# Both feed-forward blocks of a hybrid transformer kernel: inputs mixed with the previous token ahead of the products, residual sums on GpSimd

## The chip, the cores and the metric

The kernel runs on one core of a Trainium2 chip. The metric is the device time of one execution in microseconds (us), where less is better. The engines are named as the profile names them: PE (TensorE), its weight loads PEld, DVE (VectorE), ACT (ScalarE), POOL (GpSimd) and SP (SyncE, which issues the transfers). Each runs its own list of instructions in order, and they wait for each other by semaphores.

## The reference

The input x has 2 sequences of 2048 tokens with 128 features, all float32. Four blocks follow each other, each added to x after a layernorm: causal attention with one head of 128 and rotary embedding, the FFN, a linear attention with 16 heads of 64 and a decaying state, and the same FFN with the same weights again. The change is to the FFN:

```python
def ffn(x, W_r, W_k, W_v, mu_r, mu_k):
    x_prev = concatenate([zeros, x[:, :-1, :]], axis=1)    # the token before
    xr = mu_r * x + (1 - mu_r) * x_prev                    # mu: one factor per feature
    xk = mu_k * x + (1 - mu_k) * x_prev
    r = sigmoid(xr @ W_r.T)
    k_act = square(relu(xk @ W_k.T))
    return r * (k_act @ W_v.T)
```

## The kernel before

The program is a row of phases: projections, attention, the first FFN (ffn_phase, lines 782 to 994), and the linear phase (linear_phase, from line 1314), into whose last steps the last FFN (class LastFfn, from line 1179) is woven. At the end of a phase all engines meet before the next one starts. X holds all tokens in SBUF from start to end.

An FFN works on 8 groups of 512 tokens (4 tiles of 128), even groups from the first sequence, odd ones from the second. A group goes through these steps, which both FFNs have under the same names:

- moments (DVE, lines 92 to 100), roots (POOL, 102 to 107: variance plus eps, then the power of -0.5) and normalize (DVE, 109 to 113: four pieces) give the normed tokens, two groups of buffers.
- turn (PE): four transposes to a PSUM bank, so that features lie in the partitions. copy_x (ACT) copies it to xT, 513 columns wide: column 0 is the last token of the group before in the same sequence, kept by a one-column copy. So the token before is the same buffer shifted by a column.
- copy_x also rounds xT to x_hi, and low_part (POOL) subtracts x_hi from xT to get x_lo. The keys are exact to more than the fast format fp32r by three products hi*hi, hi*lo, lo*hi.
- keys (PE): W_k is held twice, times mu and times 1 - mu (FfnWeights.vector, 761 to 770, at the attention's start, with wk_hi and wk_lo made from both). For each of the two shifts there are three matmuls over 512 columns, six in all. receptance (PE): four blocks of 128 tokens, for each one a float32 product with x and W_r*mu and one with the token before and W_r*(1 - mu), eight in all. A float32 matmul shows as two passes in the profile.
- tanh (ACT) gives the gate from the receptance, as sigmoid is half of 1 + tanh of the half. square (ACT): Relu and then Square of the keys. values (PE): four float32 products with W_v.
- output (DVE): gated = (tanh + 1) * values, then X = gated + X. In the last FFN, SP stores each group's tokens when its sum is there (eight transfers of 256 KB).

The first FFN runs the groups in slots. In slot k, DVE has normalize(k+1), moments(k+2), output(k-2); PE has turn(k), receptance(k-1), values(k-2), keys(k-1); ACT has copy_x(k), tanh(k-1), square(k-1) and some exponentials for tables of the linear phase (eight each in slots 0 and 1, four each in slots 6 and 7); POOL has low_part(k), roots(k+2), and in slot 7 the product of a table of 128x1024 (line 1145). In slot 8, DVE first scales the output weights (line 1174) and norms the first two tiles for the linear phase. Each of the four PSUM results has two banks.

The last FFN has one bank for each result, borrowed from the linear attention, and its order is written out by hand on each engine (lines 1702 to 1733, 1887 to 1912, 2070 to 2090, 2190 to 2199). Between its steps stand those of the linear phase's last token tile: square_u (ACT) and sum_squares (PE) sum the outputs' squares, add_totals, turn_totals and gather_totals bring them to invert_totals (POOL, a power of -0.5), turn_scales, copy_scales and spread_scales bring the factors back, scale_u, high_u and low_u apply and split, project_out (PE, 24 matmuls), copy_y, turn_y and residual add them to X. Groups 6 and 7 hold the last tile of their sequence, so their moments can't start before that residual.

## Time and profile before

| | us |
|---|---|
| time before, median of 3 runs | 908.69 (906.55 to 910.41) |
| the profiled execution's own time | 905.67 |
| its span, first to last instruction | 901.5 |
| PE, DVE, ACT, POOL busy | 814.4, 556.2, 570.5, 584.7 |
| mean granted clock of PE | 0.981 |

The span is what the trace covers; the time of the same execution holds some 4 us around it. Busy times are sums over the span, and a busy engine is one with an instruction at work, a blocked one included. A granted clock of 1.00 is TensorE's full speed (2.4 GHz), 0.5 its lower level (1.2 GHz).

### The profile page before, as it was taken

Reading aid. Unit: us, or ns where it says so; the run is one execution under the profiler, and the core shown is the slowest. Engines: PE = TensorE matmul, PEld = TensorE weight load, DVE = VectorE, ACT = ScalarE, POOL = GpSimd, SP = SyncE. Lnnn points to the kernel's source line nnn. Section 1 sums busy time; section 2 is a strip of 40 time slices with the busy share of each in tenths; the row PEclk is TensorE's granted clock in tenths of the full one; section 3 lists DMA queues with packets and bytes.
Section 4 is the critical chain, followed back from the end, with each engine's and each line's share of the span. In section 5 each row is a group of like instructions: output and inputs, shape, how many; then the busy total and the mean of one; then the engine's idle time right before and its main releaser. Section 6 shows DMA issues by size and latency. Waiting matters only on the chain.

```text
span 901.5 us, 31429 instructions
## 1 busy us (share of the span) xinstructions
PE 814.4 (90%) x13280; PEld 707.7 (79%) x13280; DVE 556.2 (62%) x1296; ACT 570.5 (63%) x1202; POOL 584.7 (65%) x514
## 2 busy tenths in 40 slices
PE   4958998999797799999999999999999999996977
PEld 3647997899696687888788888888888887875866
DVE  3976666566684356567467466567467566567463
ACT  4746554655565666767767767767767767664544
POOL 4983211320445888977977967977977977977332
PEclk9988999999998899999999999999999999999999
DMA  5101000100100000000000000000000000000011
...
DMA packets 19417, 12.38 MB, mean 14 GB/s; under 512 B 7760, under 2 KB 18768, under 8 KB 19024
## 3 DMA queue, kind: packets, MB, share of 16 engines
...
## 4 chain that ended last, share of the span: by engine, by line
PE 55%; POOL 4%; DVE 4%; issue 3%; ACT 2%; DVEq 0%; POOLq 0%; ACTq 0%
PE la_ps L1465 9%; PE la_ps L1467 8%; PE la_ps L1466 8%; PE la_o_ps L1528 4%; PE la_o_ps L1544 4%; PE la_s_ps L1558 3%; PE la_ps L1575 3%; PE la_ps L1509 3%; PE la_ps L1496 2%; PE la_ps L1609 2%; PE la_ps L1610 2%; PE la_ps L1611 2%; DVE la_u L1765 1%; POOL la_scale L2141 1%; PE la_ps L1598 1%
## 5 line engine op out<-in xcount | busy, mean ns | idle before, releaser
L2109 POOL TENSOR_TENSOR la_coef<-la_ssk,lt_mhalf 128x32 f32<-128x32 f32 x16 | 87.1, 5442 | 70.2 <-DVE la_ssk L1782 70.2
L1465 PE MATMUL la_ps<-la_x_hi,w_hi 128*128 128x256 f32 x384 | 115.0, 300 | 1.8 <-ACT la_v L1922 1.7
L1467 PE MATMUL la_ps<-la_x_hi,w_lo 128*128 128x256 f32 x384 | 107.5, 280 | 0.4 <-issue 0.4
L1466 PE MATMUL la_ps<-la_x_lo,w_hi 128*128 128x256 f32 x384 | 107.3, 279 | 0.0
L2141 POOL TENSOR_TENSOR la_scale<-la_scale,lt_mhalf 128x32 f32<-128x32 f32 x16 | 99.9, 6241 | 6.8 <-DVE la_scale L1758 6.8
L1805 DVE TENSOR_TENSOR lt_state<-la_s_ps,la_faded 128x512 f32<-128x512 f32 x62 | 42.6, 686 | 70.0 <-PE la_o_ps L1544 57.6
L1465 PEld LDWEIGHTS la_ps<-la_x_hi,w_hi 128*128 128x128 f32 x384 | 72.2, 188 | 11.2 <-issue 6.2
L713 ACT ACTIVATE at_probs<-at_s_ps,at_ntop 128x512 f32<-128x512 f32 (+2 forms) x80 | 49.0, 623 | 46.5 <-DVE at_ntop L655 46.4
L598 PE MATMUL at_o_ps<-V,at_probsT 128*128 128x128 f32 x544 | 74.5, 277 | 3.2 <-DVE at_probsT L507 2.0
L531 POOL CAST at_q_hi<-qk_hi 128x128 fp32r<-128x128 f32 x32 | 9.4, 294 | 104.6 <-PE at_s_ps L572 102.2
L598 PEld LDWEIGHTS at_o_ps<-V,at_probsT 128*128 128x128 f32 x544 | 68.9, 192 | 6.4 <-ACT at_probsT L729 2.3
L1466 PEld LDWEIGHTS la_ps<-la_x_lo,w_hi 128*128 128x128 f32 x384 | 72.3, 188 | 0.7
L1467 PEld LDWEIGHTS la_ps<-la_x_hi,w_lo 128*128 128x128 f32 x384 | 72.2, 188 | 0.6 <-issue 0.6
L1943 ACT ACTIVATE la_gate<-la_ps,lt_bias_g 128x256 f32<-128x256 f32 x128 | 50.1, 483 | 34.7 <-PE la_ps L1467 34.7
L2135 POOL TENSOR_TENSOR la_faded<-lt_state,lt_decay_s 128x512 f32<-128x512 f32 x62 | 64.2, 1046 | 7.3 <-DVE lt_state L1805 7.1
L1742 DVE TENSOR_TENSOR la_pT<-la_ps,lt_decay 128x512 f32<-128x512 f32 x64 | 41.1, 683 | 41.7 <-PE la_ps L1509 41.7
L2127 POOL TENSOR_TENSOR la_k<-la_k,lt_decay_k 128x1024 f32<-128x1024 f32 x32 | 61.0, 1906 | 4.8 <-ACT n_xn L1992 4.8
L1465 PE MATMUL la_ps<-w_hi,la_x_hi 128*128 128x512 f32 x128 | 57.1, 446 | 7.1 <-POOL la_x_lo L2100 4.3
L2119 POOL TENSOR_TENSOR la_v<-la_v,la_coef 128x1024 f32<-128x1024 f32 x32 | 60.3, 1905 | 1.3
L1943 ACT ACTIVATE la_f<-la_ps,lt_bias_f 128x256 f32<-128x256 f32 x128 | 51.6, 473 | 13.7 <-PE la_ps L1467 12.4
L1922 ACT ACTIVATE la_k<-la_ps 128x512 f32<-128x512 f32 x64 | 38.4, 600 | 30.5 <-PE la_ps L1467 27.7
L1544 PE MATMUL la_o_ps<-la_qdT,lt_state 64*64 64x64 f32 x2048 | 45.7, 222 | 8.7 <-issue 5.9
...
## 6 DMA issues: line engine op xcount, KB each, us to landing
...
```

The source lines that it names most:

```text
L598: mm = eng.matmul(o_ps[n % 2][:, 0:P], probsT[:, (BLK[n] + j) % 2, t * P:(t + 1) * P], V[:, bass.ds(b * NT + kt, 1), :], start=(kt == 0), ...
L713: eng.activation(probs[:, n % 2, j * G:j * G + width], s_ps[:, k * G:k * G + width], ACT.Exp, bias=ntop[:, n % 2, 1:2], scale=1.0 / C, acc ...
L1465: eng.matmul(out, l_hi, r_hi, start=True, stop=False)
L1466: eng.matmul(out, l_hi, r_lo, start=False, stop=False)
L1467: return eng.matmul(out, l_lo, r_hi, start=False, stop=True)
L1544: mm = eng.matmul(o_ps[h % 2][rows, part(i, c)], state[own, b, h // 2, :], qdT[own, b, h // 2, chunk(c)], start=False, stop=True, skip_gro ...
L1943: act = eng.activation(where[:, c, :], ps[bank][:, r * W:(r + 1) * W], ACT.Tanh, bias=bias[:, c:c + 1], scale=0.5)
L2109: eng.tensor_tensor(coef[:, :], ssk[:, :], mhalf[:, :], ALU.pow).then_inc(s["coef_step"], 1)
L2119: eng.tensor_tensor(own, own, over_d(coef[:, b * H:(b + 1) * H]), ALU.mult).then_inc(s["vb_ready"], 1)
L2127: eng.tensor_tensor(own, own, over_d(decay_k[:, :]), ALU.mult).then_inc(s["kd_ready"], 1)
L2135: eng.tensor_tensor(faded[:, b, :, :], state[:, b, :, :], over_e, ALU.mult).then_inc(s["faded_second" if c else "faded_first"], 1)
L2141: eng.tensor_tensor(scale[:, :, :], scale[:, :, :], powers, ALU.pow).then_inc(s["scale_step"], 1)
```

## The change

- FfnWeights keeps W_k and W_r as they are. The products with mu and 1 - mu go (four operations on DVE), wk_hi and wk_lo have half the size, and 1 - mu (rest) is kept as a factor per feature.
- A new ACT step, rests, makes xk and xr as the token before times 1 - mu, by two scaled copies of 512 columns. A new DVE step, mix, adds x times mu to each. xk is split by high_part (ACT, was part of copy_x) and low_part (POOL, or DVE for group 2 of the last FFN); both are 512 columns wide.
- keys has three matmuls and not six, receptance four and not eight.
- output is split into gate (DVE) and residual, which is on POOL, apart from groups 0 and 7 of the last FFN, where DVE does it. Relu and Square work in one buffer, and the gate writes over the tanh.
- Both FFNs are one class, Ffn. In a slot of the first one DVE has normalize(k+1), mix(k), moments(k+2), gate(k-2); ACT has copy_x(k), rests(k), tanh(k-1), high_part(k), square(k-1) and the exponentials; POOL has low_part(k), roots(k+2), residual(k-2).
- In the last FFN the order is rewritten on each engine. low_part(1) is now behind invert_totals on POOL, keys(1), turn(3), values(1), receptance(2) and keys(2) are ahead of turn_scales on PE.

```diff
     def vector(self, eng):
-        w, mu, rest, wk, wr = self.w, self.mu, self.rest, self.wk, self.wr
         eng.wait_ge(self.loaded, 32)
-        eng.tensor_scalar(rest[:, :], mu[:, :], -1.0, 1.0, ALU.mult, ALU.add).then_inc(self.rest_ready, 1)
-        eng.tensor_scalar(wk[:, 0, :], w[:, 1, :], mu[:, 1:2], None, ALU.mult).then_inc(self.scaled, 1)
-        eng.wait_ge(self.rest_ready, 1)
-        eng.tensor_scalar(wk[:, 1, :], w[:, 1, :], rest[:, 1:2], None, ALU.mult).then_inc(self.scaled, 1)
-        eng.tensor_scalar(wr[:, 0, :], w[:, 0, :], mu[:, 0:1], None, ALU.mult).then_inc(self.scaled, 1)
-        eng.tensor_scalar(wr[:, 1, :], w[:, 0, :], rest[:, 0:1], None, ALU.mult).then_inc(self.scaled, 1)
-        eng.tensor_scalar(self.wv[:, :], w[:, 2, :], 0.5, None, ALU.mult).then_inc(self.scaled, 1)
+        eng.tensor_scalar(self.rest[:, :], self.mu[:, :], -1.0, 1.0, ALU.mult, ALU.add).then_inc(self.scaled, 1)
+        eng.tensor_scalar(self.wv[:, :], self.w[:, 2, :], 0.5, None, ALU.mult).then_inc(self.scaled, 1)
     def scalar(self, eng):
-        eng.wait_ge(self.scaled, 2)
-        eng.activation(self.wk_hi[:, :, :], self.wk[:, :, :], ACT.Copy).then_inc(self.wk_hi_ready, 1)
+        eng.wait_ge(self.loaded, 32)
+        eng.activation(self.wk_hi[:, :], self.w[:, 1, :], ACT.Copy).then_inc(self.wk_hi_ready, 1)
     def gpsimd(self, eng):
         eng.wait_ge(self.wk_hi_ready, 1)
-        eng.tensor_tensor(self.wk_lo[:, :, :], self.wk[:, :, :], self.wk_hi[:, :, :].bitcast(F32),
-                          ALU.subtract).then_inc(self.wk_lo_ready, 1)
...
+class Ffn:
...
+    def keys(self, eng, g):
+        w, hi, lo = self.weights, self.x_hi[:, g % 2, :], self.x_lo[:, g % 2, :]
+        eng.wait_ge(self.lo_ready[g % 2], g // 2 + 1)
+        ps = self.bank(eng, "k", g, self.k_pos_ready)
+        eng.matmul(ps[:, :], w.wk_hi[:, :], hi, start=True, stop=False)
+        eng.matmul(ps[:, :], w.wk_lo[:, :], hi, start=False, stop=False)
+        eng.matmul(ps[:, :], w.wk_hi[:, :], lo, start=False, stop=True).then_inc(self.k_full, 1)
+    def receptance(self, eng, g):
+        eng.wait_ge(self.xr_ready, g + 1)
+        ps = self.bank(eng, "r", g, self.r_ready)
+        for j in range(GT):
+            part = slice(j * P, (j + 1) * P)
+            mm = eng.matmul(ps[:, part], self.xr[:, g % 2, part], self.weights.wr, start=True, stop=True)
+        mm.then_inc(self.r_full, 1)
...
+    def mix(self, eng, g):
+        x, mu = self.xT[:, g % 2, 1:1 + G], self.weights.mu
+        for k, (own, ready) in enumerate(((self.xk, self.xk_ready), (self.xr, self.xr_ready))):
+            eng.wait_ge(self.rest_ready, 2 * g + k + 1)
+            eng.scalar_tensor_tensor(own[:, g % 2, :], x, mu[:, 1 - k:2 - k], own[:, g % 2, :], ALU.mult, ALU.add).then_inc(ready, 1)
+    def gate(self, eng, g):
+        eng.wait_ge(self.r_ready, g + 1)
+        eng.wait_ge(self.o_full, g + 1)
+        own, banks = self.r_act[:, g % 2, :], self.banks["o"]
+        eng.scalar_tensor_tensor(own, own, 1.0, banks[g % len(banks)][:, :], ALU.add, ALU.mult).then_inc(self.gated_ready, 1)
+    def copy_x(self, eng, g):
+        b, banks = g % 2, self.banks["xt"]
+        eng.wait_ge(self.xt_full, g + 1)
+        if g == 0:
+            eng.wait_ge(self.carried, 1)
+        if g >= 2:
+            eng.wait_ge(self.xk_ready, g - 1)
+            eng.wait_ge(self.xr_ready, g - 1)
+            eng.activation(self.xT[:, b, 0:1], self.xT[:, b, G:G + 1], ACT.Copy).then_inc(self.carried, 1)
+            eng.wait_ge(self.carried, g)
+        eng.activation(self.xT[:, b, 1:1 + G], banks[g % len(banks)][:, :], ACT.Copy).then_inc(self.xt_ready, 1)
+    def rests(self, eng, g):
+        b, rest = g % 2, self.weights.rest
+        eng.wait_ge(self.xt_ready, g + 1)
+        if g >= 2:
+            eng.wait_ge(self.lo_ready[g % 2], g // 2)
+        eng.activation(self.xk[:, b, :], self.xT[:, b, 0:G], ACT.Copy, scale=rest[:, 1:2]).then_inc(self.rest_ready, 1)
+        if g >= 2:
+            eng.wait_ge(self.r_full, g - 1)
+        eng.activation(self.xr[:, b, :], self.xT[:, b, 0:G], ACT.Copy, scale=rest[:, 0:1]).then_inc(self.rest_ready, 1)
+    def high_part(self, eng, g):
+        eng.wait_ge(self.xk_ready, g + 1)
+        if g >= 2:
+            eng.wait_ge(self.k_full, g - 1)
+        eng.activation(self.x_hi[:, g % 2, :], self.xk[:, g % 2, :], ACT.Copy).then_inc(self.hi_ready, 1)
...
+    def low_part(self, eng, g):
+        eng.wait_ge(self.hi_ready, g + 1)
+        eng.tensor_tensor(self.x_lo[:, g % 2, :], self.xk[:, g % 2, :], self.x_hi[:, g % 2, :].bitcast(F32),
+                          ALU.subtract).then_inc(self.lo_ready[g % 2], 1)
+    def residual(self, eng, g):
+        eng.wait_ge(self.gated_ready, g + 1)
+        eng.tensor_tensor(self.tokens(g), self.r_act[:, g % 2, :].rearrange("p (t c) -> p t c", t=GT), self.tokens(g),
+                          ALU.add).then_inc(self.x_ready[g % 2], 1)
...
+        @block.vector
+        def _(eng):
+            for k in range(N + 2):
+                if k == N:
+                    tables.vector(eng)
+                    for g in range(2):
+                        eng.wait_ge(ffn.x_ready[g], 1)
+                    next_norm.first_vector(eng)
+                if has(k + 1) and k + 1 >= 2:
+                    ffn.normalize(eng, k + 1)
+                if has(k):
+                    ffn.mix(eng, k)
+                if has(k + 2):
+                    ffn.moments(eng, k + 2)
+                if has(k - 2):
+                    ffn.gate(eng, k - 2)
+        @block.scalar
+        def _(eng):
+            for k in range(N + 2):
+                if has(k):
+                    ffn.copy_x(eng, k)
+                    ffn.rests(eng, k)
+                if has(k - 1):
+                    ffn.tanh(eng, k - 1)
+                if has(k):
+                    ffn.high_part(eng, k)
+                if has(k - 1):
+                    ffn.square(eng, k - 1)
...
+                if has(k):
+                    ffn.low_part(eng, k)
+                if has(k + 2):
+                    ffn.roots(eng, k + 2)
+                if k == N:
+                    next_norm.first_gpsimd(eng)
+                if has(k - 2):
+                    ffn.residual(eng, k - 2)
...
             for m in STEPS[:-1]:
                 step(m)
+            eng.wait_ge(s["u_ready"], 2 * B * NT)
+            ffn.receptance(eng, 0)
             eng.wait_ge(up_read[0], B * NT)
             ffn.keys(eng, 0)
             sum_squares(NT, "su")
             ffn.turn(eng, 2)
             turn_totals(NT)
-            eng.wait_ge(s["u_ready"], 2 * B * NT)
-            ffn.receptance(eng, 0)
-            ffn.keys(eng, 1)
             ffn.values(eng, 0)
             ffn.receptance(eng, 1)
+            ffn.keys(eng, 1)
             ffn.turn(eng, 3)
+            ffn.values(eng, 1)
+            ffn.receptance(eng, 2)
+            ffn.keys(eng, 2)
             turn_scales(NT)
             for j in range(4):
                 spread_scales(NT, j)
-            ffn.keys(eng, 2)
-            ffn.receptance(eng, 2)
-            project_out(NT)
-            ffn.values(eng, 1)
             ffn.values(eng, 2)
-            turn_y(NT)
             ffn.receptance(eng, 3)
             ffn.keys(eng, 3)
+            project_out(NT)
             ffn.turn(eng, 4)
             ffn.values(eng, 3)
-            for g in range(4, ffn.GROUPS):
-                if g + 1 < ffn.GROUPS:
-                    ffn.turn(eng, g + 1)
-                ffn.receptance(eng, g)
-                if g > 4:
-                    ffn.values(eng, g - 1)
-                ffn.keys(eng, g)
-            ffn.values(eng, ffn.GROUPS - 1)
+            turn_y(NT)
+            ffn.receptance(eng, 4)
+            ffn.turn(eng, 5)
+            ffn.keys(eng, 4)
+            ffn.values(eng, 4)
+            ffn.receptance(eng, 5)
+            ffn.turn(eng, 6)
+            ffn.keys(eng, 5)
+            ffn.values(eng, 5)
+            ffn.receptance(eng, 6)
+            ffn.turn(eng, 7)
+            ffn.keys(eng, 6)
+            ffn.receptance(eng, 7)
+            ffn.values(eng, 6)
+            ffn.keys(eng, 7)
+            ffn.values(eng, 7)
...
+            ffn.mix(eng, 1)
             ffn.normalize(eng, 3)
-            ffn.output(eng, 0)
+            ffn.moments(eng, 4)
+            ffn.mix(eng, 2)
+            ffn.gate(eng, 0)
+            ffn.residual(eng, 0)
+            ffn.low_part(eng, 2)
+            ffn.moments(eng, 5)
+            ffn.mix(eng, 3)
+            ffn.gate(eng, 1)
             for j in range(4):
                 scale_u(NT, j)
             for j in range(4):
                 low_u(NT, j)
-            ffn.moments(eng, 4)
-            ffn.output(eng, 1)
             ffn.normalize(eng, 4)
-            ffn.moments(eng, 5)
+            ffn.normalize(eng, 5)
+            ffn.gate(eng, 2)
+            ffn.mix(eng, 4)
             residual(NT)
-            ffn.normalize(eng, 5)
             taken(eng, NT, "yt")
             ffn.moments(eng, 6)
-            ffn.output(eng, 2)
-            ffn.output(eng, 3)
+            ffn.moments(eng, 7)
+            ffn.gate(eng, 3)
+            ffn.mix(eng, 5)
             ffn.normalize(eng, 6)
-            ffn.moments(eng, 7)
-            ffn.output(eng, 4)
             ffn.normalize(eng, 7)
-            for g in range(5, ffn.GROUPS):
-                ffn.output(eng, g)
+            ffn.gate(eng, 4)
+            ffn.mix(eng, 6)
+            ffn.gate(eng, 5)
+            ffn.mix(eng, 7)
+            ffn.gate(eng, 6)
+            ffn.gate(eng, 7)
+            ffn.residual(eng, 7)
...
+                    ffn.rests(eng, 1)
+                    ffn.high_part(eng, 0)
             for m in STEPS[:-1]:
                 step(m)
             square_u(LAST, 1)
+            ffn.tanh(eng, 0)
             ffn.square(eng, 0)
             ffn.copy_x(eng, 2)
-            ffn.tanh(eng, 0)
+            ffn.rests(eng, 2)
+            ffn.high_part(eng, 1)
+            ffn.tanh(eng, 1)
             ffn.square(eng, 1)
-            ffn.tanh(eng, 1)
             ffn.copy_x(eng, 3)
+            ffn.high_part(eng, 2)
+            ffn.rests(eng, 3)
+            ffn.tanh(eng, 2)
+            ffn.square(eng, 2)
             copy_scales(NT)
+            ffn.high_part(eng, 3)
             for j in range(4):
                 high_u(NT, j)
-            ffn.square(eng, 2)
-            ffn.tanh(eng, 2)
-            copy_y(NT)
             ffn.tanh(eng, 3)
             ffn.square(eng, 3)
+            copy_y(NT)
             ffn.copy_x(eng, 4)
+            ffn.rests(eng, 4)
+            ffn.high_part(eng, 4)
             for g in range(4, ffn.GROUPS):
                 if g + 1 < ffn.GROUPS:
                     ffn.copy_x(eng, g + 1)
+                    ffn.rests(eng, g + 1)
                 ffn.tanh(eng, g)
                 ffn.square(eng, g)
+                if g + 1 < ffn.GROUPS:
+                    ffn.high_part(eng, g + 1)
...
+                    eng.wait_ge(up_full[0], B * NT)
                     ffn.low_part(eng, 0)
-                    ffn.low_part(eng, 1)
             step(STEPS[0])
             tables.gpsimd_clear(eng)
             for m in STEPS[1:-1]:
                 step(m)
             invert_totals(NT)
-            ffn.low_part(eng, 2)
+            ffn.low_part(eng, 1)
             ffn.roots(eng, 4)
+            ffn.roots(eng, 5)
             ffn.low_part(eng, 3)
-            ffn.roots(eng, 5)
+            ffn.residual(eng, 1)
+            ffn.low_part(eng, 4)
+            ffn.residual(eng, 2)
             ffn.roots(eng, 6)
-            ffn.low_part(eng, 4)
             ffn.roots(eng, 7)
-            for g in range(5, ffn.GROUPS):
-                ffn.low_part(eng, g)
+            ffn.residual(eng, 3)
+            ffn.low_part(eng, 5)
+            ffn.residual(eng, 4)
+            ffn.low_part(eng, 6)
+            ffn.residual(eng, 5)
+            ffn.low_part(eng, 7)
+            ffn.residual(eng, 6)
```

## Rows read from the trace of the kernel before

**Rows 1.** The page: busy time by engine; shares of the chain that ended last.

```profile
PE 814.4 (90%) x13280; PEld 707.7 (79%) x13280; DVE 556.2 (62%) x1296; ACT 570.5 (63%) x1202; POOL 584.7 (65%) x514
...
PE 55%; POOL 4%; DVE 4%; issue 3%; ACT 2%; DVEq 0%; POOLq 0%; ACTq 0%
```

**Rows 2.** Windows: stretch; length; busy us of PE, PEld, DVE, ACT, POOL; clock; DMA.

```profile
235.50:280.60 45.10, 38.81 (x272) 33.91 (x272) 35.84 (x111) 30.36 (x73) 22.17 (x27) 1.00 0.07 13
280.60:285.00 4.40, 3.74 (x11) 2.88 (x12) 0.00 (x0) 2.59 (x5) 2.91 (x8) 0.52 0.02 6
```

**Rows 3.** Timeline, first FFN, PE: start, duration, engine, line, output<-inputs, count [idle before].

```profile
247.46 0.40 PE L973 MATMUL f_r_ps<-fw_wr,f_xT 128*128 128x128 f32 x2
...
249.26 1.06 PE L981 MATMUL f_o_ps<-fw_wv,f_k_act 128*128 128x128 f32 x8
...
250.07 0.47 PE L963 MATMUL f_k_ps<-f_x_hi,fw_wk_hi 128*128 128x512 f32 x1
...
251.56 0.75 PE L955 MATMUL f_xt_ps<-const,n_xn 128*128 128x128 f32 x4
...
252.14 0.40 PE L973 MATMUL f_r_ps<-fw_wr,f_xT 128*128 128x128 f32 x2
```

**Rows 4.** Timeline, first FFN, DVE and POOL: one turn, the first and last normalize.

```profile
240.29 2.07 DVE L112 TENSOR_SCALAR n_xn<-X,n_mv,n_rstd 128x128 f32<-128x128 f32 x4 [3.52 <-POOL n_rstd L107]
...
247.16 0.86 DVE L94 BATCH_NORM_STATS2 n_stats<-X 128x6 f32<-128x128 f32 x4
...
248.80 1.01 POOL L107 TENSOR_TENSOR n_rstd<-n_rstd,n_mhalf 128x4 f32<-128x4 f32 x1
...
249.78 1.29 POOL L855 TENSOR_TENSOR f_x_lo<-f_xT,f_x_hi 128x513 fp32r<-128x513 f32 x1
249.91 2.01 DVE L112 TENSOR_SCALAR n_xn<-X,n_mv,n_rstd 128x128 f32<-128x128 f32 x4 [0.18 <-POOL n_rstd L107]
...
263.98 2.02 DVE L112 TENSOR_SCALAR n_xn<-X,n_mv,n_rstd 128x128 f32<-128x128 f32 x4 [0.18 <-POOL n_rstd L107]
```

**Rows 5.** Groups by form, POOL (whole span), ACT (first FFN): busy us, mean ns.

```profile
L239 POOL TENSOR_TENSOR qkv_rot<-qkv_by_cos,qkv_by_sin 128x512 f32<-128x512 f32 x16 | 24.3, 1534 | 0.5 <-issue 0.3 <-DVE qkv_by_sin L278 0.2
...
L914 ACT ACTIVATE f_x_hi<-f_xT 128x513 fp32r<-128x513 f32 x8 | 5.1, 634 | 0.3
...
L1128 ACT ACTIVATE lt_decay<-lt_lag,lt_rate 128x64 f32<-128x64 f32 x16 | 4.0, 333 | 0.0
```

**Rows 6.** Timeline, end of the first FFN.

```profile
269.90 1.43 DVE L883 TENSOR_TENSOR X<-f_gated,X 128x512 f32<-128x512 f32 x1
...
270.75 2.82 POOL L1145 TENSOR_TENSOR lt_decay<-lt_decay,lt_strict 128x1024 f32<-128x1024 f32 x1
...
271.26 2.94 DVE L1174 TENSOR_SCALAR lt_w_out<-lt_w_out,lt_norm_w 128x1024 f32<-128x1024 f32 x1
...
280.68 0.57 PE L1452 MATMUL la_ps<-const,n_xn 128*128 128x128 f32 x2 [3.60 <-PEq L788]
```

**Rows 7.** Timeline, the weights' products at the attention's start, DVE.

```profile
67.03 0.38 DVE L765 TENSOR_SCALAR fw_wk<-fw_w,fw_mu 128x128 f32<-128x128 f32 x1
...
68.06 0.29 DVE L648 TENSOR_TENSOR at_s_ps<-at_s_ps,const 128x128 f32<-128x128 f32 x1
```

**Rows 8.** Timeline, the last FFN, by engine: DVE, ACT, POOL, PE.

```profile
846.11 2.14 DVE L1797 SCALAR_TENSOR_TENSOR la_u<-la_gate,la_u 128x1024 f32<-128x1024 f32 x1
...
868.97 1.11 DVE L112 TENSOR_SCALAR n_xn<-X,n_mv,n_rstd 128x128 f32<-128x128 f32 x4
...
898.07 0.69 DVE L1270 TENSOR_TENSOR X<-f_gated,X 128x512 f32<-128x512 f32 x1
...
846.23 1.06 ACT L2006 ACTIVATE la_sq<-la_u 128x1024 f32<-128x1024 f32 x1 [0.42 <-DVE la_u L1791]
...
850.36 5.46 POOL L2141 TENSOR_TENSOR la_scale<-la_scale,lt_mhalf 128x32 f32<-128x32 f32 x1 [3.20 <-DVE la_scale L1758]
...
863.49 0.39 PE L1609 MATMUL la_ps<-la_u_hi,lt_w_out_hi 128*128 128x256 f32 x1 [1.16 <-DVE la_u_lo L1771]
```

400 lines of the change are left out of this document (112 added, 288 removed).

## The prediction

> **What bounds the kernel now.** I read the page first. PE is busy 90% of the span, and it also has 55% of the chain of waits that ended last [rows 1]. A reader could stop there and price the change by PE's saving. But the change touches two stages only, some 45 us after the attention (the first FFN) and the last 50 us, so I went on to the stretches of time. In the first FFN PE is busy 38.81 of 45.10 us, DVE 35.84, ACT 30.36, POOL 22.17, at full granted clock [rows 2]. The timeline of one group shows PE without a gap: receptance starts at 247.46, values at 249.26, keys at 250.07, the next turn at 251.56, the next receptance at 252.14, so 4.68 us a group [rows 3]. The same timeline shows a second bound at par with it, a loop between DVE and POOL: moments start on DVE at 247.16, the power of the roots runs on POOL from 248.80, and the next normalize starts at 249.91, 2.75 us behind the moments. Its four pieces take 2.01 us, though four undisturbed ones take 1.11 [rows 4, 8]: POOL's low_part started at 249.78 with 1.29 us, just ahead of them, and the first piece had to sit it out. 2.75 + 2.0 is 4.75: the normalize of a group waits for the one before it as much as for PE.
>
> **The first FFN, part by part.** PE: receptance goes from 8 to 4 matmuls, keys from 6 to 3. Receptance took 1.80 us and keys 1.49 [rows 3], so 0.90 and 0.70 us go, 1.6 us a group, and PE has about 3.1 us of work in it. ACT: two scaled copies (rests) come in, x_hi moves behind the mix as high_part. One 128x513 SBUF copy takes 634 ns [rows 5], and independent ones follow each other by about 0.55 (estimate); ACT goes from some 3.0 to 4.1 us a group. DVE: two mixes come in, the residual sum goes out. The nearest row is the residual sum of the same size, 0.69 us [rows 8]; back to back I take 1.25 us for both mixes (bounds 1.2, and 2.5 if each meets a POOL operation). POOL takes the residual: the nearest row is the 128x512 sum of two SBUF tensors at L239, 1534 ns in the mean with disturbance [rows 5], low_part has 1.29 undisturbed; I take 1.27 (bounds 1.05 to 1.6).
>
> Now the loop. DVE's order becomes normalize(k+1), mix(k), moments(k+2), gate(k-2). The roots of k+2 wait for moments(k+2), normalize(k+2) waits for the roots, and the mix stands between normalize and moments. So the loop is normalize 1.03 (start to start of four undisturbed pieces and what follows, inside the 1.11 of [rows 8]) + mix 1.25 + the 2.75 of [rows 4] = 5.03 us. Two things are added. POOL's residual(k-2) comes right behind the roots, its gate being done by then (0.7 us behind the moments, where the roots take 1.4), so it has started when the normalize arrives and costs it 1.17, as low_part does today. And low_part(k) now waits for mix and high_part: it ends about 0.1 us after the moments, ahead of the roots on POOL. That is 6.3 us for a full turn, against 4.75. PE (3.1) and ACT (4.1) fit within it and save nothing.
>
> In time: today normalize(2) starts at 240.29 and normalize(7) at 263.98, five turns of 4.74 later [rows 4]. After: mix(0) can't start before ACT has copied and scaled group 0 and low_part(0) moves back with it, so normalize(2) starts about 241.7. The next turn is free of a residual (5.15); the third waits for ACT, whose eight exponentials of a slot (x16 in 4.0 us, [rows 5]) now stand ahead of the rests (6.1); three turns of 6.3 follow: normalize(7) at 271.9, +7.9.
>
> The end of the stage: mix(7) waits for rests(7), which stand on ACT behind high_part(6), square(5) and four exponentials: 278.7. high_part and low_part(7) follow until 281.6. Then POOL has residual(5), the 128x1024 product at L1145, the roots for the next phase, and residuals 6 and 7. L1145 took 2.82 from 270.75, of which DVE's residual at 269.90 (1.43, itself held until POOL was done) was ahead for 0.54; so 2.3. DVE's L1174 took 2.94, held till L1145 ended [rows 6]; it works 0.65. Summed: residual(5) to 283.4 (behind L1174), L1145 to 285.7, roots of 1.0 and 0.9 to 287.9, normalizes to 288.6, gates 6 and 7 to 290.1, residual(7) at 290.7 to 291.9. Today the next phase's first matmul is at 280.68 [rows 6], 0.3 us behind the last residual; both end in a barrier. So +11.5 us. Bounds: +6 if no residual blocks and the end hides on ACT's side, +14 if mixes are blocked too.
>
> **Weights.** Four products of weights with mu leave DVE, 67.03 to 68.06 without wv and rest, just ahead of the attention's first mask [rows 7], where PE stands idle: -0.8 us (bounds -1.0 and 0). The wk_hi and wk_lo operations halve beside other work: nothing.
>
> **The last FFN.** Its groups lie between steps of the linear phase's last chain. I followed the new order by hand with the durations above. The sums of x: rests(0) and mix(0) fall in idle time of ACT and DVE. After copy_x(1), ACT now also has rests(1) and high_part(0) ahead of square_u: 846.23 becomes 846.8 [rows 8]. low_part(0), today long done, can start only at 846.95. DVE's gate_u, which today starts at 846.11 and is held to 2.14 us by a low_part [rows 8], is then first, and holds low_part(0) until 847.3; it ends at 848.6. keys(0) stands ahead of the sum of squares on PE and waits for it, then takes 0.8. So the power of the totals starts on POOL at 852.3, not 850.36 [rows 8]: 2.0 late.
>
> The larger delay is behind it. low_part(1) stood ahead of invert_totals on POOL; now it stands behind, so it waits out the 5.46 us power and its two followers (to 858.45) and ends at 859.75. PE holds keys(1), turn(3), values(1), receptance(2) and keys(2) ahead of turn_scales. keys(1) ends 860.65, Relu and Square on ACT 862.0, values(1) and receptance(2) 863.9, and keys(2) waits for low_part(2) on DVE (copy_x(3) and high_part(2) are behind the Square) until 864.1. turn_scales follows at 864.9, the spread at 866.7, scale_u and low_u to 872.2: project_out starts at 872.25, not 863.49 [rows 8], +8.8.
>
> Given back: with groups 0 to 2 done and group 3 nearly so, what comes behind is shorter. turn_y ends 877.05, rests and mix of group 4 hold residual(NT) until 878.7, moments 6 and 7 to 881.65, roots to 883.9, normalizes to 888.0 (residual(3) and low_part(5) get in between their pieces). turn(7) stands behind values(5) and receptance(6): 892.0. From there one chain: copy 1.5 with the start, rests and mix to 894.9, high_part behind tanh(6) and square(6) 896.9, low_part 898.3, keys 899.2, Relu and Square 900.5, values 901.6, gate and residual 903.1. Today the last residual ends at 898.76 [rows 8]: +4.3 us. Bounds: -5 if PE's 1.6 us per group count here after all, +9.
>
> PE idles some 5.5 us before keys(1). An idle of 3.60 us before 280.68 today has a granted clock of 0.52 behind it, the lower level of 1.2 GHz [rows 2, 6]. keys(1), values(1) and receptance(2) would then take up to twice their time, and about 1.5 us of it falls on the chain; I add that (bounds 0 and 3).
>
> **Sum.** +11.5 - 0.8 + 4.3 + 1.5 = +16.5. The profiled execution had a span of 901.5 and a time of 905.67, 3 us under the median of 908.69; the sum gives a span of 918 and 922.2 by that execution, 925 by the median. I take 924.
>
> **Rivals.**
> A, PE was the bound, 897: in the tail DVE's gate waits for PE, and PE is busy 90% [rows 1]. If each of the last seven groups gives back 1.6 us (11 us) and the first FFN falls to DVE's own work of 4.4 us a group (normalize 1.1, mixes 1.3, moments 1.3, gate 0.7; -1.5), the kernel gets faster by 12. It decides if the moments' loop has slack, which [rows 4] speak against: the normalize starts as soon as the roots are there. 9%.
> B, the residual on POOL doesn't hold the normalize up: turns of 5.1, the first FFN at +6, in all +11: 920. Against it is the 2.01 for 1.11 [rows 4, 8]. 15%.
> The Trainium skill, "Perfetto Trace Analysis", section "Optimizing Scalar/DVE Operations", warns that moving work between GpSimd and DVE may not help as they share an SBUF port; by it B does not come about and the sum stays at +16.5 and not +11, and the 2.01 agrees.
> C, the clock: PE is busy half of each turn in the first FFN. If the grant falls to 1.2 GHz there and through the tail, PE needs 6.2 us a group, at par with the loop, and keys, values and turns lengthen the closing chains: +7 more, 932. For it is the 0.52 of [rows 2], against it that PE's idle time in a turn is cut into pieces of under 2 us by turn, receptance, values and keys. 10%.
> D, loss and gain cancel: the first FFN +5, the tail -5, 909. 11%.
> The forecast itself: 55%, its own range 917 to 930.
>
> Half a per cent, 4.5 us, is what a measurement here can tell from no change. Faster: A and a little of D, 0.10. Same: the middle of D, 0.07. Slower: 0.83. The range of 910 to 932 leaves out A, half of D and the upper end of C.
>
> **What would show it.** In the first FFN: normalize starts 6.3 us apart, residuals on POOL starting right at the roots' end with a first normalize piece of 1.2 to 1.3 beside them, PE idle near half. Its end near 292. In the tail: low_part(1) behind the power, PE idle from 854 to 860, project_out near 872 to 874, the last residual near 903. It is wrong if the normalizes start under 5 us apart, or if project_out starts before 866.

## The result, and the profile after

| | before | after |
|---|---|---|
| time, median of 4 runs each | 907.62 us (904.08 to 910.41) | 929.11 us (927.22 to 929.91) |
| profiled execution: time, span | 905.67, 901.5 | 927.22, 924.9 |
| PE, DVE, ACT, POOL busy | 814.4, 556.2, 570.5, 584.7 | 808.7, 563.8, 589.5, 599.4 |
| mean granted clock of PE | 0.981 | 0.958 |

The changed kernel takes 1.0237 of the time before (95% interval 1.0205 to 1.0269): 21 us more. Run again later beside the kernel before, it had 926.55 against 905.46 us, 1.0241 (1.0210 to 1.0271). The forecast was 924 with 910 to 932.

The page says where not to look: PE's busy time fell by 5.7 us although half of its products in both FFNs went, and PE's share of the chain that ended last rose from 55% [rows 1] to 57%.

```profile
PE 808.7 (87%) x13104; PEld 696.5 (75%) x13104; DVE 563.8 (61%) x1311; ACT 589.5 (64%) x1234; POOL 599.4 (65%) x527
...
PE 57%; DVE 3%; ACT 3%; issue 3%; POOL 2%; DVEq 0%; POOLq 0%; ACTq 0%
```

Two marks cut the 23.4 us that the span grew by: x_lo, POOL's first operation on the tokens of the linear phase, and gate_o, DVE's first operation on the last outputs of the linear attention. The first x_lo of the linear phase starts at 292.00 instead of 282.09: +9.9, of which the attention's first mask gives back 0.5 (67.56 instead of 68.06, [rows 7]), so the first FFN itself is +10.4. The last step's gate_o starts at 854.09 instead of 844.91: +9.2, so the linear phase gave back 0.7. From that gate_o to the end of the last residual it is 68.06 us instead of 53.85: +14.2. Nearly all lies in the two stretches that the change touches.

The timeline of DVE in the first FFN, to be read against [rows 4] (start, duration, engine, line, operation, shape, and in brackets idle time and its releaser; L112 is normalize, L863 mix, L94 the first half of moments, L869 gate):

```profile
246.22 1.11 DVE L112 TENSOR_SCALAR n_xn<-X,n_mv,n_rstd 128x128 f32<-128x128 f32 x4 [1.51 <-POOL n_rstd L107]
...
252.35 1.99 DVE L112 TENSOR_SCALAR n_xn<-X,n_mv,n_rstd 128x128 f32<-128x128 f32 x4 [1.09 <-POOL n_rstd L107]
254.26 0.74 DVE L863 SCALAR_TENSOR_TENSOR f_xk<-f_xT,fw_mu,f_xk 128x512 f32<-128x512 f32 x1
254.92 0.74 DVE L863 SCALAR_TENSOR_TENSOR f_xr<-f_xT,fw_mu,f_xr 128x512 f32<-128x512 f32 x1
255.59 0.86 DVE L94 BATCH_NORM_STATS2 n_stats<-X 128x6 f32<-128x128 f32 x4
...
256.78 0.66 DVE L869 SCALAR_TENSOR_TENSOR f_r_act<-f_r_act,f_o_ps 128x512 f32<-128x512 f32 x1
258.38 1.99 DVE L112 TENSOR_SCALAR n_xn<-X,n_mv,n_rstd 128x128 f32<-128x128 f32 x4 [0.94 <-POOL n_rstd L107]
```

And POOL beside it (L923 is low_part, L107 the roots' power, L928 the residual sum):

```profile
255.74 1.27 POOL L923 TENSOR_TENSOR f_x_lo<-f_xk,f_x_hi 128x512 fp32r<-128x512 f32 x1 [2.26 <-ACT f_x_hi L899]
...
257.25 1.02 POOL L107 TENSOR_TENSOR n_rstd<-n_rstd,n_mhalf 128x4 f32<-128x4 f32 x1
258.24 1.27 POOL L928 TENSOR_TENSOR X<-f_r_act,X 128x512 f32<-128x512 f32 x1
```

One turn is 258.38 - 252.35 = 6.03 us, and it can be added up from the starts: normalize to mix 1.91, both mixes to moments 1.33, moments to the next normalize 2.79. Before it was 4.7 [rows 4]. The residual sum starts at 258.24, just ahead of the normalize, and the four pieces take 1.99 us; at 246.22, with no sum on POOL, they take 1.11.

The last FFN, PE (L1449 is the sum of squares, L829 opens keys(1), L846 is values: of group 0 at 862.12, of group 1 at 873.89, of groups 4, 5 and 7 in the last three lines; L1472 is the spread, L1483 opens project_out):

```profile
859.33 1.89 PE L1449 MATMUL la_ps<-la_sq,lt_pick 128*32 128x256 f32 x16
...
862.12 1.06 PE L846 MATMUL la_o_ps<-fw_wv,f_k_act 128*128 128x128 f32 x8
...
870.90 0.79 PE L829 MATMUL la_s_ps<-f_x_hi,fw_wk_hi 128*128 128x512 f32 x1 [5.34 <-POOL f_x_lo L923]
...
873.89 2.07 PE L846 MATMUL la_o_ps<-fw_wv,f_k_act 128*128 128x128 f32 x8 [0.49 <-ACT f_k_act L915]
...
880.25 1.21 PE L1472 MATMUL la_ps<-la_scT,lt_spread 128*128 128x256 f32 x8 [1.40 <-ACT la_scT L1858]
...
885.80 0.39 PE L1483 MATMUL la_ps<-la_u_hi,lt_w_out_hi 128*128 128x256 f32 x1 [1.86 <-DVE la_u_lo L1652]
...
898.02 1.59 PE L846 MATMUL la_o_ps<-fw_wv,f_k_act 128*128 128x128 f32 x8 [3.19 <-ACT f_k_act L915]
...
906.07 2.08 PE L846 MATMUL la_o_ps<-fw_wv,f_k_act 128*128 128x128 f32 x8 [3.22 <-ACT f_k_act L915]
...
918.78 1.84 PE L846 MATMUL la_o_ps<-fw_wv,f_k_act 128*128 128x128 f32 x8 [1.35 <-ACT f_k_act L915]
```

Here two things are to be seen: the wait of 5.34 us for low_part(1) behind the power, and durations that vary for one and the same work: the eight matmuls of values take 1.06 us at 862.12 and 2.07 at 873.89. The windows say why (stretch, length, busy us and count of PE, PEld, DVE, ACT, POOL, then the granted clock, DMA share, GB/s):

```profile
860.00:870.00 10.00, 4.29 (x34) 2.73 (x26) 7.75 (x22) 3.92 (x8) 6.74 (x4) 0.84 0.01 2
870.00:880.00 10.00, 7.46 (x28) 6.19 (x28) 3.75 (x13) 5.56 (x11) 4.03 (x5) 0.59 0.09 27
880.00:890.00 10.00, 7.89 (x62) 7.41 (x63) 7.54 (x17) 5.67 (x12) 2.52 (x2) 1.00 0.09 26
890.00:900.00 10.00, 4.79 (x31) 4.07 (x30) 8.81 (x30) 6.47 (x12) 7.30 (x8) 0.93 0.10 28
900.00:910.00 10.00, 6.78 (x32) 6.30 (x31) 3.87 (x7) 4.25 (x8) 4.09 (x4) 0.67 0.17 52
910.00:925.00 15.00, 6.83 (x34) 5.06 (x32) 3.48 (x5) 6.01 (x11) 2.83 (x3) 0.73 0.18 52
```

Before, the clock was 1.00 in every window from 840 to 890, as in this one:

```profile
870.00:880.00 10.00, 7.66 (x58) 6.95 (x57) 8.02 (x36) 5.18 (x10) 3.67 (x5) 1.00 0.25 72
```

After, it is low for most of 870 to 880 (0.59) and of 900 to 910 (0.67), and for part of all other windows but one. Ahead of gate_o it is low for a while in both kernels (0.81 from 830 to 840 before, 0.66 from 840 to 850 after); no run prices that. Note the trap in these rows: PE's busy time in 870 to 880 is 7.46 us for 28 matmul records, and in 880 to 890 7.89 for 62. A slow PE looks busy.

### The profile page after: what moved, and what is told of

Read it like the earlier page. It is cut to its first block, busy times and chain, and to the rows that moved or that the text cites. A ratio compares the mean times of both kernels' runs of the same rounds, so it can differ in the third digit from the quotient of the medians.

```text
span 924.9 us, 31149 instructions
## 1 busy us (share of the span) xinstructions
PE 808.7 (87%) x13104; PEld 696.5 (75%) x13104; DVE 563.8 (61%) x1311; ACT 589.5 (64%) x1234; POOL 599.4 (65%) x527
## 4 chain that ended last, share of the span: by engine, by line
PE 57%; DVE 3%; ACT 3%; issue 3%; POOL 2%; DVEq 0%; POOLq 0%; ACTq 0%
PE la_ps L1339 10%; PE la_ps L1340 8%; PE la_ps L1341 8%; PE la_o_ps L1402 4%; PE la_o_ps L1418 4%; PE la_ps L1449 3%; PE la_s_ps L1432 3%; PE la_ps L1383 3%; PE la_ps L1370 2%; PE la_ps L1483 2%; PE la_ps L1484 2%; PE la_ps L1485 2%; DVE la_u L1646 1%; PE la_ps L1472 1%; PE la_o_ps L846 1%
## 5 line engine op out<-in xcount | busy, mean ns | idle before, releaser
L1836 ACT ACTIVATE la_f<-la_ps,lt_bias_f 128x256 f32<-128x256 f32 x128 | 51.5, 472 | 13.8 <-PE la_ps L1341 12.4
L923 POOL TENSOR_TENSOR f_x_lo<-f_xk,f_x_hi 128x512 fp32r<-128x512 f32 x15 | 19.1, 1273 | 60.0 <-ACT f_x_hi L899 60.0
```

The source lines that it names most:

```text
L1836: act = eng.activation(where[:, c, :], ps[bank][:, r * W:(r + 1) * W], ACT.Tanh, bias=bias[:, c:c + 1], scale=0.5)
```

## The experiments

Ratios are to runs of the kernel before on the same chip. "Tail" is the time from the last step's gate_o to the end of the last residual in the profiled execution (before 53.85, after 68.06, after once more 68.00). Each kernel's theory is quoted as it stood before the run.

### One half at a time

`old_first` has the first FFN as before and the last one as changed:

```
-    ffn_phase(nc, X, const, weights, norm_1, tables, norm_2)
+    ffn_phase(nc, X, const, weights.split, norm_1, "f1_", tables=tables, next_norm=norm_2)
```

> The first FFN as it was, the last FFN as changed; the weights are made in both forms, some 0.8 us more on VectorE at the attention phase's start. Theory (where the traces put the time): the last FFN alone costs 13 to 14 us, so the time is that of before plus 14 to 15, 921 to 923. Rival (the sum of the prediction: 5.8 us for the last FFN and the clock): 913 to 915. A third: a part of the changed tail's loss comes from the pressure of both changes together, and this kernel shows less than 10.

Measured: 919.28 us against 905.28, ratio 1.0165 (1.0139 to 1.0191).

`old_last` has the first FFN as changed and the last one as before:

> The first FFN as changed, the last FFN as it was. Theory: the first FFN costs what its own stretch shows, 9.5 to 10 us, and nothing of it comes back later: 917 to 918. Rival: what the first FFN loses is given back in the linear phase or its tail, under 5 us: 908 to 913. With the kernel above the two losses should add up to the whole, 21 to 23 us; if they don't, the halves act on each other.

Measured: 916.33 against 905.28, ratio 1.0127 (1.0095 to 1.0159). Both kernels make the weights in both forms. normalize(2) starts at 242.50 instead of 240.29 in the one, at 243.64 instead of the changed kernel's 241.06 in the other, so 2.2 and 2.6 us are lost ahead of either FFN, more than the 0.8 us expected. The first mask is no later than before (68.00 and 67.76), so they are lost within the attention phase: from its first mask to its last it takes 152.2 and 152.3 us, where the kernels before and after have 150.1 and 150.3. The granted clock is 0.83 there from 150 to 160 in both, and 1.00 in the kernels before and after. It doesn't take the weights in two forms: `filled` (below) has the changed kernel's weights and attention, and shows the same, 152.0 us. The window of the changed kernel and that of `filled`:

```profile
150.00:160.00 10.00, 8.20 (x54) 6.78 (x55) 7.99 (x36) 5.49 (x16) 3.67 (x12) 1.00 0.02 5
```

```profile
150.00:160.00 10.00, 8.07 (x47) 7.02 (x47) 7.50 (x34) 4.58 (x14) 3.66 (x12) 0.83 0.01 2
```

As they stand, the halves come to 14.0 + 11.1 = 25.1 us, against 21 to 22 for the whole. Without the 2.2 and 2.6 they come to 11.8 + 8.5 = 20.3, so the losses add within their intervals, as far as one profile of each can say. The tail is 68.17 us in `old_first`: nearly all of its loss is made by the last FFN alone, and not by how late it starts. It is 55.48 in `old_last`, whose last FFN is as before. That is 1.6 us over the 53.85 of before, all of it behind residual(NT), where the clock is 0.85 from 880 to 890: a tail of the same code differs by so much from one kernel to the next. The rival of 5.8 us for the last FFN and the clock falls.

### The clock in the tail

The next kernel is the changed one with matmuls that nothing reads, on PE where it stood idle:

```
+    def fill(self, eng, what, g, read, n):
+        ps = self.bank(eng, what, g, read)
+        for j in range(n):
...
+            eng.matmul(ps[:, part], self.weights.wv[:, :], self.const[:, C_IDENT:C_IDENT + P], start=True, stop=True)
...
+            ffn.fill(eng, "k", 1, ffn.k_pos_ready, 24)
             ffn.keys(eng, 1)
```

> The changed kernel with matmuls of 128x128 that nothing reads, put in the last FFN on TensorE where it stood idle (each in a PSUM bank that the next product overwrites; the output is unchanged). Theory: TensorE's clock fell to 0.59 to 0.74 in four stretches of the tail because it had little to do, and this cost 5 to 9 us: the granted clock is over 0.9 in 860 to 920, values(1) takes 1.06 us and not 2.07, and the time is 920 to 924. Rival: the low clock lies beside longer chains on VectorE and ScalarE and costs under 2 us: 927 to 930. A third: the added matmuls stand in the way of the real ones and make it slower, 930 to 934.

Measured: 926.33 against 905.28, ratio 1.0240 (1.0210 to 1.0270), no gain in the time. The trace shows the clock at 1.00 from 850 to 910, as wanted, and a tail of 65.08 us, 3.0 less than in the changed kernel. It isn't more because the added matmuls run past the moment at which the real inputs are there. And 1.7 us of the gain are lost again in the attention phase, at the clock of 0.83 shown above. So the same kernel with fewer of them:

```
-            ffn.fill(eng, "k", 1, ffn.k_pos_ready, 24)
+            ffn.fill(eng, "k", 1, ffn.k_pos_ready, 20)
-            ffn.fill(eng, "xt", 4, ffn.xt_ready, 12)
+            ffn.fill(eng, "xt", 4, ffn.xt_ready, 5)
-            ffn.fill(eng, "o", 4, ffn.gated_ready, 20)
+            ffn.fill(eng, "o", 4, ffn.gated_ready, 8)
...
```

> As the kernel with matmuls that nothing reads, with fewer of them. There the granted clock was 1.00 from 850 to 910 and values(1) took 1.16 us, and still the ratio was 1.024, as without them. But they stood in the way in places: project_out started 1.5 us after its last input, values(4) 2.5 us and values(5) 1.1 us after square's end, receptance(7) 1.5 us after mix. Here the counts are cut so that they end before the inputs do. Theory (the clock's fall costs 5 to 8 us, which the waits took back): ratio 1.015 to 1.018 to before. Rival (the clock's fall costs 1 to 3 us, since the products at half speed stood beside ScalarE's and VectorE's chains): 1.020 to 1.023.

Measured: 919.17 against 905.16, ratio 1.0164 (1.0141 to 1.0188), and a tail of 59.93 us instead of 68.06. Its windows, its sum of squares (L1456) and its values(1) (L853):

```profile
850.00:860.00 10.00, 8.41 (x179) 6.46 (x177) 5.47 (x11) 7.03 (x15) 1.29 (x1) 1.00 0.01 2
860.00:870.00 10.00, 9.09 (x79) 8.59 (x76) 7.75 (x22) 3.61 (x7) 7.83 (x6) 1.00 0.10 28
870.00:880.00 10.00, 7.69 (x58) 6.73 (x58) 6.52 (x18) 8.22 (x16) 5.43 (x5) 1.00 0.01 2
880.00:890.00 10.00, 9.54 (x79) 9.11 (x78) 7.32 (x20) 5.35 (x10) 1.04 (x1) 1.00 0.09 26
890.00:900.00 10.00, 8.52 (x62) 7.13 (x61) 9.50 (x28) 7.21 (x14) 8.11 (x9) 1.00 0.19 54
900.00:910.00 10.00, 7.42 (x59) 6.67 (x58) 3.54 (x6) 6.15 (x12) 4.02 (x4) 1.00 0.18 52
```

```profile
858.99 1.07 PE L1456 MATMUL la_ps<-la_sq,lt_pick 128*32 128x256 f32 x16
...
872.05 1.16 PE L853 MATMUL la_o_ps<-fw_wv,f_k_act 128*128 128x128 f32 x8 [0.91 <-ACT f_k_act L922]
```

No work was taken out and no order changed, only idle time of PE filled, and 8.1 us went from the tail, some 6.6 us (0.0073 of the time) from the kernel. The low clock costs the tail that much. The first form shows how narrow the gap is: with its misplaced matmuls (project_out 1.5 us late, values(4) 2.5, values(5) 1.1, receptance(7) 1.5) the tail kept 3.0 of these 8.1 us.

### The order in the tail

```
             ffn.normalize(eng, 3)          # VectorE
+            ffn.low_part(eng, 1)
             ffn.moments(eng, 4)
...
             invert_totals(NT)              # GpSimd
-            ffn.low_part(eng, 1)
             ffn.roots(eng, 4)
```

> The changed kernel with one operation of the tail moved: low_part(1) from GpSimd behind the power of 128x32 (5.9 us) to VectorE behind normalize(3) (0.7 us). Theory: keys(1) waited 5.3 us for it and everything up to turn_scales, project_out and residual(NT) stood behind keys(1) on TensorE; keys(1) starts at about 866, turn_scales at the power's end near 870, and the last residual comes 7 to 9 us earlier: 920 to 922. Rival: the clock's fall and the chain of ScalarE take most of it back: 925 to 929.

Measured: 916.73 against 905.28, ratio 1.0129 (1.0095 to 1.0163), some 10 us less than the changed kernel; tail 59.86, 8.2 us less. The rest lies ahead of gate_o, where the edit changes nothing: it starts at 852.91 instead of 854.09. In its timeline, PE:

```profile
864.84 0.50 PE L829 MATMUL la_s_ps<-f_x_hi,fw_wk_hi 128*128 128x512 f32 x1 [0.47 <-DVE f_x_lo L923]
...
872.37 1.21 PE L1472 MATMUL la_ps<-la_scT,lt_spread 128*128 128x256 f32 x8 [1.40 <-ACT la_scT L1859]
...
877.92 0.39 PE L1483 MATMUL la_ps<-la_u_hi,lt_w_out_hi 128*128 128x256 f32 x1 [1.86 <-DVE la_u_lo L1652]
```

keys(1) starts 11.9 us behind gate_o (852.91 here) instead of 16.8, project_out 25.0 instead of 31.7. One operation of 0.7 us, moved, gave more than the wait of 5.34 us in front of it. By keys(1) it has given 4.9; the next 1.7 come from values(1) and receptance(2), which take 1.13 and 1.06 us and not 2.07 and 1.92. The granted clock is at 1.00 again from 860 to 890 without any added matmul:

```profile
860.00:870.00 10.00, 6.53 (x50) 5.51 (x47) 9.75 (x28) 6.91 (x13) 7.85 (x5) 1.00 0.04 11
870.00:880.00 10.00, 6.74 (x50) 5.85 (x49) 9.39 (x26) 6.64 (x12) 5.00 (x5) 1.00 0.15 42
880.00:890.00 10.00, 4.91 (x38) 4.20 (x37) 7.25 (x29) 6.80 (x14) 5.20 (x6) 1.00 0.09 26
```

With `filled_less`, where the same idle time is filled, this shows that the idle time in front of keys(1) is what brought the clock down behind it.

### The order in the first FFN

```
                 if has(k + 1) and k + 1 >= 2:
                     ffn.normalize(eng, k + 1)
-                if has(k):
-                    ffn.mix(eng, k)
                 if has(k + 2):
                     ffn.moments(eng, k + 2)
+                if has(k):
+                    ffn.mix(eng, k)
```

with roots(k+2) ahead of low_part(k) on GpSimd in the same way.

> The changed kernel with two pairs exchanged in each slot of the first FFN: VectorE's moments(k+2) ahead of mix(k), GpSimd's roots(k+2) ahead of low_part(k). Theory: a turn is 6.0 us because moments(k+2) to the next normalize holds mix(k) (1.4 us) ahead of the chain moments, roots, normalize; with mix beside roots a turn is 4.9 to 5.3 us and the phase 5 to 6 us shorter, the time 921 to 924 where the changed kernel has 927 to 929. Rival: VectorE is full with or without the order (its own instructions with the blocked normalize are 5.7 us a group), a turn stays at 5.8 to 6.0 and the time within 2 us. A third: low_part behind roots makes keys late, and TensorE and ScalarE then set the turn, 6 us or more.

Measured: 928.08 against 905.16, ratio 1.0245 (1.0209 to 1.0280): no gain in the time, and not quite for one of the reasons given. Its timeline, POOL and DVE:

```profile
256.67 1.26 POOL L923 TENSOR_TENSOR f_x_lo<-f_xk,f_x_hi 128x512 fp32r<-128x512 f32 x1
256.80 2.98 DVE L112 TENSOR_SCALAR n_xn<-X,n_mv,n_rstd 128x128 f32<-128x128 f32 x4 [0.39 <-POOL n_rstd L107]
257.90 1.28 POOL L928 TENSOR_TENSOR X<-f_r_act,X 128x512 f32<-128x512 f32 x1
...
259.70 0.86 DVE L94 BATCH_NORM_STATS2 n_stats<-X 128x6 f32<-128x128 f32 x4
...
261.75 1.41 POOL L107 TENSOR_TENSOR n_rstd<-n_rstd,n_mhalf 128x4 f32<-128x4 f32 x1
...
263.26 2.97 DVE L112 TENSOR_SCALAR n_xn<-X,n_mv,n_rstd 128x128 f32<-128x128 f32 x4 [0.39 <-POOL n_rstd L107]
```

With low_part behind the roots, both of POOL's 128x512 operations stand beside the normalize, whose pieces now take 2.98 us. The turn is 6.46 us, not 5. The mix left the chain (1.33 us), and two things came into it: the second operation on POOL (1.0 us), and roots that take longer beside the mixes. Their power takes 1.41 us and not 1.02, and from the moments to the next normalize it is 3.56 us and not 2.79. DVE is idle for 0.39 us of such a turn, so the rival that VectorE is full was close.

The phase as a whole still got shorter, by 0.6 us from the attention's last mask to x_lo (73.5 instead of 74.1), because the first normalizes start earlier. The time does not show it: the attention phase before it took 1.5 us more in this profile (151.8, at 0.83 from 150 to 160).

### The residual sum in the first FFN

```
                 if has(k - 2):
                     ffn.gate(eng, k - 2)            # VectorE
+                    ffn.residual(eng, k - 2)
```

> The changed kernel with the residual sums of the first FFN on VectorE behind the gate, not on GpSimd (those of the last FFN as changed). Theory: the sum on GpSimd costs VectorE about 0.9 us a turn where it stands beside normalize (1.99 us for the four pieces, not 1.11), and the sum on VectorE costs 0.7 us there but 0.5 of it beside roots, which the next normalize waits for anyway: a turn of 5.2 to 5.5 us instead of 6.0, 3 to 5 us faster than the changed kernel. Rival: the 0.7 us moves onto the engine that is the bound, a turn of 5.9 to 6.2 and the time within 1.5 us.

Measured: 923.86 against 905.16, ratio 1.0217 (1.0193 to 1.0240). The interval overlaps that of the changed kernel, so the time alone doesn't settle it. The trace does:

```profile
251.80 1.11 DVE L112 TENSOR_SCALAR n_xn<-X,n_mv,n_rstd 128x128 f32<-128x128 f32 x4 [0.36 <-POOL n_rstd L107]
```

normalize takes 1.11 us in every turn, turns take 5.14, and the first x_lo of the next phase is at 287.58 instead of 292.00, 4.4 us earlier. Of these, 0.5 lie ahead of the attention's first mask (67.03 for 67.56), so the sum's place is worth 3.9 us.

The same part of the change alone, on the kernel before (its other parts left out):

```
+            def residual(g):                        # GpSimd, behind the roots
+                eng.wait_ge(gated_ready, g.count(1, AHEAD + 1))
+                eng.tensor_tensor(tokens(g), gated[:, g.b, :].rearrange("p (t c) -> p t c", t=GT), tokens(g), ALU.add).then_inc(x_ready, 1)
```

> The kernel before with one part of the change done alone: the first FFN's residual sums on GpSimd, in the same place as in the changed kernel; no mixing ahead of the products. Theory: VectorE loses 0.7 us of its own a turn and gains some 0.9 us of standing still beside the sum, so a turn goes from 4.7 to 4.8 to 5.0 us and the kernel is 0 to 3 us slower (1.000 to 1.004). Rival: VectorE gets free, but TensorE is at 10.0 of 10 us there, so the turn stays at 4.7 and the ratio at 1.000. A third: VectorE was the bound and the sum is hidden on GpSimd, 3 to 5 us faster, 0.995.

Measured: 908.50 against 905.46, ratio 1.0044 (1.0023 to 1.0064). POOL and DVE in its timeline (L859 is the sum, L855 low_part):

```profile
260.88 1.29 POOL L859 TENSOR_TENSOR X<-f_gated,X 128x512 f32<-128x512 f32 x1
261.02 2.99 DVE L112 TENSOR_SCALAR n_xn<-X,n_mv,n_rstd 128x128 f32<-128x128 f32 x4 [0.91 <-POOL n_rstd L107]
262.12 1.28 POOL L855 TENSOR_TENSOR f_x_lo<-f_xT,f_x_hi 128x513 fp32r<-128x513 f32 x1
```

The sum left DVE (0.69 us) and the turn grew from 4.70 to 5.66 us, more than the 0.1 to 0.3 expected; the ratio is at the upper end of what was. The 0.69 us that DVE was spared bought it 0.98 us of standing still, and they were no gain: before, the sum ran beside the roots, for which the next normalize waits anyway.

### All of it together

The changed kernel with the sums of the first FFN on VectorE, low_part(1) of the tail on VectorE, and added matmuls where PE still stood idle:

> The changed kernel with what helped put together: the first FFN's sums on VectorE (its last phase ended 4.4 us earlier), low_part(1) of the tail on VectorE (10 us), and matmuls that nothing reads where TensorE still stood idle in the tail (6.7 us alone, less here, since with low_part(1) moved the clock is 1.00 from 860 to 890 anyway). Theory: what is left is the first FFN's longer turns (5.1 against 4.7 us, and its longer end, 5.5 us in all) and the tail's longer chain at full clock (0 to 3 us): 1.005 to 1.010, and it doesn't beat the kernel before. Rival: the three overlap, and it stays at low_part(1)'s own 1.012. A third, that it beats the kernel before, needs the tail to be shorter than before, under 1.003.

Measured: 911.20 against 905.46, ratio 1.0069 (1.0044 to 1.0094), tail 55.62. On the same chip, the changed kernel unaltered:

> The changed kernel once more, beside the two others on the same chip, so that they can be compared with it and not only by way of the kernel before: ratio 1.0237 within its interval.

Measured: 1.0241 (1.0210 to 1.0271). So some 15 of the 21 us come back without giving up the mixing. Of what remains, 6.3 us lie in the first FFN, counted from the attention's last mask to x_lo (70.2 instead of 63.9). By x_lo alone (287.51 instead of 282.09) it is 5.4, because the first mask comes 1.1 us earlier here. Of the 1.8 us in the tail, `old_last` shows that 1.6 can be there with the last FFN as before.

A combination of the two orders was tried as well:

> The exchange in the first FFN's slots together with low_part(1) of the last FFN on VectorE. If the two act apart, the gains add: 10 us of low_part(1) (ratio 1.0129 against 1.0237 of the changed kernel) and what the exchange gives by itself, 1.006 to 1.008 of before where the exchange gives 5 to 6 us, 1.012 where it gives none. Rival: the tail's gain hangs on where the linear phase starts, and they don't add.

Measured: 920.71 against 905.16, ratio 1.0175 (1.0155 to 1.0195), over the 1.0129 for low_part(1) alone. By the expectation the sum asked for 1.013, as the exchange had given nothing in the time. Of the 2.5 us by which the span is longer than that of `low_one` (918.0 against 915.5), 1.7 lie in the tail, 61.54 us instead of 59.86, where the order is the same and the granted clock is 0.75 from 900 to 910 instead of 0.95; the other 0.8 lie ahead of gate_o, and none of them in the first FFN, which is 0.6 us shorter here too. So whether the two act apart isn't shown by the time. The traces show each of them at its own place, and a clock in the tail that isn't the same from one kernel to the next.

Last, the first FFN as before with the mended tail:

> The first FFN as before, and the last FFN as in the kernel that put three together (low_part(1) on VectorE, and matmuls that nothing reads in TensorE's idle stretches). Theory: of that kernel's 6 us over the kernel before, 5.4 lay in the first FFN and 1.8 in the tail (gate_o to the last sum 55.6 us against 53.9), so this one is at 1.001 to 1.004: the mixing in the last FFN, well placed, costs 0.5 to 3 us and gains nothing. Rival (a version that beats both): the tail's 1.8 us were of that one profile, and it is at 0.996 to 0.999. A third: 1.005 or more, and the first FFN's loss was hidden in part.

Measured: 906.77 against 905.38, ratio 1.0010 (0.9995 to 1.0026), tail 55.65. normalize(2) is 1.7 us late here, and again the attention phase has 151.9 us and 0.83 from 150 to 160. That is no measurable difference from the kernel before; no version beats it.

## Why the prediction was right, and where a term was not

The forecast, slower by the first FFN's loop and by the order in the tail, came about: 929 measured, 924 forecast. Step by step:

**First FFN, the loop: right.** The parts were predicted as 2.2 (normalize with the blocked piece), 1.25, 2.75 and 0.1, in all 6.3 us; they measured 1.91, 1.33, 2.79 and nothing, 6.03. PE's share in it was higher than forecast, 7.0 of 10 us busy where "near half" was to be idle, which changed nothing, as PE doesn't set the turn. The residual sum on POOL took the predicted 1.27 us and started at the roots' end. It blocks the normalize by 0.88 us, not 1.17. normalize(7) starts at 270.43, where 271.9 was forecast.

**Its end: right.** From normalize(7) on, +3.5 us where +3.6 was forecast, by mix(7) at 277.36 (278.7), low_part(7) to 280.28 (281.6), the 128x1024 product in 2.35 us (2.3) and the last residual to 290.14 (291.9). In all +10.4 for +11.5. The weights gave 0.5 for 0.8 in this profile. The nine profiles with the changed weights alone have the first mask at 66.91 to 67.56, and `sum_alone`, with the old ones, has it at 67.61 and not at 68.06, so the term can't be told finely.

**Last FFN, the order: right, and to be seen only at full clock.** Microseconds behind gate_o:

| | before | forecast | filled, clock 1.00 | after |
|---|---|---|---|---|
| the totals gathered | 5.2 | 7.2 | 7.2 | 8.8 |
| spread of the scales | 13.0 | 21.8 | 22.1 | 26.2 |
| residual(NT) | 26.3 | 33.8 | 34.3 | 38.3 |
| last residual's end | 53.9 | 58.2 | 59.9 | 68.1 |

The third column of numbers is `filled_less`, which has the changed kernel's order and no low clock from 850 to 910. The hand-followed order holds within 0.5 us up to residual(NT), and its term of +4.3 us measures +6.1.

**The clock in the tail: the term that was mis-sized.** "About 1.5 us of it falls on the chain; I add that (bounds 0 and 3)." It measured 8.1 us (68.06 - 59.93). The price of one low stretch was not far off: between the gather and residual(NT) the changed kernel loses 2.4 us to it. What I missed is that it doesn't happen once. The forecast had one idle stretch, before keys(1). In the trace the sum of squares before it is already slow (1.89 us for 1.07; 1.6 us lost by the gather), and behind residual(NT) it is slow again, 1.59 and 2.08 us for the eight matmuls of values(4) and values(5), 1.84 for values(7), which costs 4.1 us. I should have followed PE's lighter load on through the tail: it is idle in pieces of 2 to 3 us there (3.19 us before values(4) at 898.02, 3.22 before values(5) at 906.07).

**The sum.** Forecast and measured, in microseconds of the span: first FFN +11.5 and +10.4, weights -0.8 and -0.5, the linear phase up to gate_o nothing and -0.7, order +4.3 and +6.1, clock +1.5 and +8.1, in all +16.5 and +23.4. The first FFN and the linear phase hid 1.8 us of the clock's miss. That 929.1 still lies in the forecast's own range of 917 to 930 is luck to that extent.

**The rivals.** A, PE the bound: PE's busy time in 255 to 265 fell from 10.00 to 7.01 us and the turn grew; false. B, the sum on POOL doesn't block: 1.99 against 1.11 us, and 3.9 us back in `sum_on_dve`; false. The Trainium skill, "Perfetto Trace Analysis", section "Optimizing Scalar/DVE Operations", warns that moving operations between GpSimd and VectorE might not help, as they share an SBUF port. The traces agree with it: 1.11, 1.99 and 2.98 us for the four pieces with none, one and two operations of GpSimd beside them, and a turn 0.96 us longer in `sum_alone`. C, the clock: right for the tail, where its +7 was closer than my 1.5, and wrong for the first FFN's loop, where the windows show 0.92, 1.00 and 0.95 from 245 to 275 and the turns from 252.35 on have the same 6.03 us. At the end of that phase the clock did fall (0.84 from 275 to 285, 0.50 from 285 to 295), which no run prices. The true run was the forecast's first FFN with C's tail. D, loss and gain cancel: false.

The two causes in the tail share a part. Either remedy alone takes 8.1 or 8.2 us off, both together 12.4 (55.62): low_part(1)'s wait was both a delay and the idle time that lowered the clock.

What stays open: why the clock falls between 150 and 160 in the attention phase of five of the fourteen profiles (`filled`, `mix_behind`, `old_first`, `old_last`, `tail_mended`), with 1.5 to 2.1 us lost each time, and why it differs in the tail between `low_one` and `both_orders`. That the added matmuls help by the clock alone rests on the granted clock and on the durations of the matmuls; no experiment told another effect of theirs apart.
